# Layer 1's experts as a sorted, grouped product instead of a dense one, in a two-layer transformer kernel

## The chip, the cores and the metric

The kernel runs on one core of one Trainium2 chip. A core has TensorE (matrix products, called PE in the profile; its weight loads are PEld), VectorE (DVE), ScalarE (ACT), GpSimd (POOL) and SyncE (SP, which issues transfers). Each engine works through its own queue in order, and semaphores tie the queues together. The metric is the device time of one execution in microseconds (us), smaller is better. The input is fixed.

## The reference, cut to what matters

The input x is 4 batches of 1024 tokens of 128 elements, in F32. Layer 0 adds a multi-query attention and a SwitchHead attention with expert-wise values and outputs; both kernels compute it in the same way. Layer 1 is a linear attention with exponential features and, beside it, a mixture of experts. Both read the same normalised xn:

```python
logits = xf @ gate_w + gate_b                 # 4096 tokens, 8 experts
top_w, top_i = top_k(logits, 2)
combine = (softmax(top_w)[:, :, None] * one_hot(top_i, 8)).sum(axis=1)
for e in range(8):
    h = gelu(xf @ w1[e] + b1[e])              # 128 -> 512
    out = out + combine[:, e:e+1] * (h @ w2[e] + b2[e])   # 512 -> 128
shared = gelu(xf @ ws1 + bs1) @ ws2 + bs2
x = x + attention(xn) + out + shared
```

Only two of the eight routed experts have a weight other than zero for a token.

## The kernel before, in words

`build` (L2203) runs three stages with a barrier between them, then stores x whole. `layer0` computes layer 0, layer 1's normalised input xnT (turned, tokens in columns) and the gates. In it the VectorE functions `choose_experts` and `mix` with the helper `top2` (L130) find the two experts and write `combine`, 128 x 32 tiles x 10. Its SyncE queue loads head weights (L643, L652) and each step's queries (L635) over 32 steps of some 80 us. `load_experts` (L1544) loads the weights of all nine experts (the shared one is the ninth) and splits w1 into an upper and a lower part. `main1` (L1572) is layer 1.

`main1` takes the batches one after the other, each in 18 slots u (`UNITS` = 2 x 9). A slot holds one expert unit, expert u % 9 on token block u // 9 of 512 tokens: `hidden` (L1793) in two halves of six split products (`matmul3`, L76: upper x upper, upper x lower, lower x upper, one pass each, on lines L79, L80 and L81), `gelu` on ScalarE (L2074), `output` (L1804) one slot later in plain F32 (two instructions each, L1810), `mix` on VectorE (L1964), which multiplies with the combine weights, and `add_mixed` on GpSimd (L2157), which adds to x.

The attention is dealt out by hand over the same slots: projections and values in slots 0 and 1, `key_peaks` in 2 to 5 and `query_peaks` in 6 to 9 (VectorE takes their maxima, L1901 and L1925), `key_halves` in 8, `key_features` in 9 to 12, `query_shift` in 10, which needs GpSimd's `square_q` of slot 9, `sum_keys` in 10 to 13, `query_features` in 13 to 16, `turn_kv` in 14 with VectorE's `mask_kv`, `weigh` in 15 and 17, each followed by VectorE's `divide` (L1957 to L1961) into oT, and `project`, in 17 and in slot 0 of the next batch. GpSimd's `add_attn` adds the result to x. GpSimd also splits the next batch's x (`lower_x`, slot 15).

TensorE's results go to a ring of three tiles (`Ring`, two banks each). `claim` takes the next tile and waits until the result that was in it three claims before has been taken out. So the order of claims ties TensorE to the readers of the tiles.

## Time and profile before

| | |
|---|---|
| median of 3 runs | 3594.96 us (3593.2 to 3598.66) |
| the profiled execution | 3593.13 us |
| its span, first to last instruction | 3591.4 us |
| TensorE busy / weight loads | 3299.4 us (92%) / 2311.3 us |
| VectorE, ScalarE, GpSimd busy | 2363.4, 1687.0, 1755.3 us |
| mean granted TensorE clock | 0.967 |
| DMA packets, bytes | 115927, 79.23 MB |

The busy time of an engine is the sum of its instructions' times, and a busy TensorE is not TensorE at its peak, since matmuls overlap. A view by stretch gives these times for a part of the span, with the clock that TensorE was granted there (1.00 is 2.4 GHz, 0.50 is 1.2 GHz). The columns of a view by stretch are: stretch, its us, then busy us and (count) of PE, PEld, DVE, ACT and POOL, the granted clock, the share of busy DMA engines, GB/s. In a view in order of time a row is start us, us, engine, line, operation, output<-inputs, shapes, count, and in brackets the idle time before it and who ended it. A view of lines groups instructions of one form, with their mean time, and with the engine's idle time before them and who ended it. Every time of the working is one of the profiled execution.

### The profile page before, as it was taken

The page shows a single profiled execution, that of the slowest core. Times are in us where ns is not written, and L with a number is a line of the kernel's source. Part 1 is how long each engine was busy: PE and PEld are TensorE (multiplying, and loading weights), DVE is VectorE, ACT ScalarE, POOL GpSimd, SP SyncE. Part 2 cuts the span into 40 slices and gives each one's busy share as a digit, 9 for nine tenths or more (in the row PEclk, how much of TensorE's full clock was granted, in tenths as well). Part 3 has the DMA queues.
Part 4 walks back from the last instruction along what each step waited for, and adds up shares of the span by engine and source line. Part 5 has one row for each costly group of instructions (what it writes and reads, how often), then busy time and mean ns, then how long its engine had stood idle before and what let it go on. Part 6 is the DMA issues. An engine that isn't in the chain of part 4 may idle for free. (4 is left out here: it accounts for less than half of the span.)

```text
span 3591.4 us, 53232 instructions
## 1 busy us (share of the span) xinstructions
PE 3299.4 (92%) x19284; PEld 2311.3 (64%) x19284; DVE 2363.4 (66%) x3586; ACT 1687.0 (47%) x2854; POOL 1755.3 (49%) x1986
## 2 busy tenths in 40 slices
PE   3899999999999999999999999999993799989897
PEld 2566666666666666666666666666662677777675
DVE  6777888787888888888888888877863212122221
ACT  1445544545554445555454544555551363534444
POOL 1466656566665566666566665665652212121111
PEclk6999999999999999999999999999996899999998
DMA  3000000001000110010000001100003000000000
GB/s 86 18 25 26 19 19 28 28 26 31 20 19 19 30 33 25 20 32 19 24 29 28 19 20 32 31 19 19 25 2 67 9 1 1 1 1 1 1 1 24
DMA packets 115927, 79.23 MB, mean 22 GB/s; under 512 B 28618, under 2 KB 104020, under 8 KB 115668
## 3 DMA queue, kind: packets, MB, share of 16 engines
q1 hardware_dynamic: 113364, 73.46, 7.6%
q10 hardware_dynamic: 2304, 2.36, 0.3%
q8 instruction: 157, 2.57, 0.3%
q14 instruction: 102, 0.84, 0.1%
HBM read 63.74 MB, written 12.06 MB: 21 GB/s over the span
## 5 line engine op out<-in xcount | busy, mean ns | idle before, releaser
L883 ACT ACTIVATE m_expA<-m_ring 128x512 f32<-128x512 f32 x1024 | 547.5, 602 | 420.5 <-PE m_ring L329 297.4
L1114 DVE TENSOR_REDUCE m_peaks<-m_ring 128x1 f32<-128x512 f32 x1024 | 653.0, 684 | 126.1 <-PE m_ring L254 119.0
L774 POOL TENSOR_TENSOR m_vprod<-m_vprod 128x512 f32<-128x512 f32 x256 | 333.5, 1303 | 622.0 <-DVE m_vprod L1127 620.7
L783 POOL TENSOR_TENSOR m_oprod<-m_oprod 128x512 f32<-128x512 f32 x256 | 327.8, 1280 | 328.5 <-DVE m_oprod L1187 328.2
L307 PE MATMUL m_ring<-m_probT,m_vs 128*128 128x256 f32 x2048 | 466.8, 381 | 1.7 <-ACT m_probT L864 1.7
L864 ACT ACTIVATE m_probT<-m_ring 128x512 f32<-128x512 f32 x512 | 284.3, 601 | 363.5 <-PE m_ring L295 333.8
L307 PEld LDWEIGHTS m_ring<-m_probT,m_vs 128*128 128x128 f32 x2048 | 391.2, 191 | 60.3 <-ACT m_probT L864 2.2
L1127 DVE TENSOR_TENSOR m_vprod<-m_ring,m_gate 128x512 f32<-128x512 f32 x512 | 341.4, 687 | 77.7 <-POOL m_vs L776 55.0
L1157 DVE TENSOR_REDUCE m_neg<-m_wide 128x1 f32<-128x1024 f32 x256 | 312.7, 1221 | 105.7 <-PE m_wide L81 105.4
L1187 DVE TENSOR_TENSOR m_oprod<-m_ring,m_go 128x512 f32<-128x512 f32 x512 | 347.0, 688 | 31.0 <-PE m_ring L81 16.5
L2161 POOL TENSOR_TENSOR k_x<-k_x,m_mixed 128x512 f32<-128x512 f32 x72 | 91.9, 1276 | 534.5 <-DVE m_mixed L1970 534.5
L2080 ACT ACTIVATE m_hT<-m_ring,l_b 128x512 f32<-128x512 f32 x288 | 182.7, 686 | 352.5 <-PE m_ring L81 352.3
L1970 DVE TENSOR_TENSOR m_mixed<-m_ring,k_combine 128x512 f32<-128x512 f32 x72 | 49.8, 692 | 450.7 <-PE m_ring L1810 450.7
L854 ACT ACTIVATE m_prob<-m_wide,m_neg 128x1024 f32<-128x1024 f32 x256 | 288.3, 1126 | 104.3 <-DVE m_neg L1157 104.3
L295 PE MATMUL m_ring<-k_ident,m_prob 128*128 128x128 f32 x2048 | 275.9, 277 | 26.9 <-DVE m_peaks L1114 26.1
L295 PEld LDWEIGHTS m_ring<-k_ident,m_prob 128*128 128x128 f32 x2048 | 233.0, 142 | 92.8 <-issue 66.3
L1810 PEld LDWEIGHTS m_ring<-l_w,m_hT 128*128 128x128 f32 x2304 | 273.6, 195 | 8.9 <-issue 2.7
L344 PE MATMUL m_sums<-m_expA,m_v 128*32 128x512 f32 x2048 | 275.1, 609 | 1.5 <-ACT m_expA L883 1.4
L1810 PE MATMUL m_ring<-l_w,m_hT 128*128 128x128 f32 x2304 | 274.2, 278 | 1.1 <-ACT m_qpT L2060 1.1
L79 PE MATMUL m_ring<-m_wvs,m_xs 128*128 128x512 f32 x512 | 237.2, 463 | 35.1 <-DVE m_oprod L1187 23.6
L254 PE MATMUL m_ring<-m_ks,m_qs 32*128 32x512 f32 x1024 | 229.4, 504 | 33.4 <-DVE m_qs L1106 28.5
L79 PE MATMUL m_wide<-m_xs,m_yT 128*128 128x512 f32 x512 | 231.0, 451 | 9.2 <-DVE m_qs L1146 5.7
(249 smaller groups left out, 6239.5 us busy)
## 6 DMA issues: line engine op xcount, KB each, us to landing
m_wraw<-in_v_w SPq DMA_DIRECT2D x32, 512.0 KB, 4.0
m_qf<-q_dram SPq DMA_DIRECT2D x128, 128.0 KB, 2.7
m_wraw<-in_o_w SPq DMA_DIRECT2D x32, 512.0 KB, 3.8
q_dram<-m_kf SPq DMA_DIRECT2D x24, 256.0 KB, 4.3
sums_dram<-m_sumsT ACTq DMA_DIRECT2D x128, 18.0 KB
m_o_in<-sums_dram SPq DMA_DIRECT2D x64, 32.0 KB
m_rden_in<-rden_dram SPq DMA_DIRECT2D x64, 32.0 KB
p_w<-in_w SPq DMA_DIRECT2D x1, 2048.0 KB, 8.3
```

Of the source, the lines that this page charges most:

```text
L79: pe.matmul(out, wh, xh, start=True, stop=False)
L295: last = pe.transpose(ps[:, c * P:(c + 1) * P], prob[t % 2][:, (4 * h + c) * P:(4 * h + c + 1) * P], ident[:, :])
L307: last = pe.matmul(ps[:, 0:2 * P], vs[n % 2][:, k, :], probT[g % 2][:, k, :], start=(k == 0), stop=(k == TPB - 1))
L774: vchain(pool.tensor_tensor(vprod[:, 0:512], vprod[:, 0:512], vprod[:, 512:1024], ALU.add))
L783: ochain(pool.tensor_tensor(op[:, 0:512], op[:, 0:512], op[:, 512:1024], ALU.add))
L854: act.activation(prob[t % 2][:, :], wide.home["scores", n, t][:, :], ACT.Exp, bias=neg[t % 2][:, :], accum_out=den[n % 2][:, t:t + 1]).the ...
L883: act.activation(expA[hh][:, c * 512:(c + 1) * 512], ring.home["scT", n, k, hh, c][:, :], ACT.Exp)\
L1114: v.tensor_reduce(peaks[:, t, hh, c:c + 1], ring.home["peaks", n, t, hh, c][:, :], AX.X, ALU.max)\
L1127: v.tensor_tensor(vprod[:, c * 512:(c + 1) * 512].rearrange("p (e d) -> p e d", e=4), ring.home["values", n, t, c][:, :].rearrange("p (e d ...
L1157: v.tensor_reduce(neg[t % 2][:, :], wide.home["scores", n, t][:, :], AX.X, ALU.max, negate=True)\
L1187: v.tensor_tensor(oprod[t % 2][:, c * 512:(c + 1) * 512].rearrange("p (e d) -> p e d", e=4), ring.home["outputs", n, t, c][:, :].rearrange ...
L1810: last = pe.matmul(ps[:, t * P:(t + 1) * P], hT[j % 2][:, k, t * P:(t + 1) * P], w2[:, e, k, :], start=(k == 0), stop=(k == HT - 1))
```

## The change

`load_experts` goes. In layer 0, `top2` keeps the two chosen ranks in `choice`, SyncE writes the normalised rows to `xn_dram` (`store_xo`) and fills the list `listed` (9984 rows of 128) with zeros. `main1` computes for each token and each of its two experts a place in that list, sorted by expert, each expert's part rounded up to groups of 256: `count_places` on TensorE counts with a triangular matrix, `rank_tokens` on VectorE sums up. GpSimd sends the rows to their places with indirect DMAs (`send_rows`, 64 of them of 128 rows of 512 bytes), and for each of 39 groups (`NG`) fetches the weights of the group's expert (`fetch_weights`, 128 rows of 4112 bytes) into one of five buffers. A group is loaded by SyncE, turned, multiplied with w1 in plain F32, put through gelu and multiplied with w2, and its answers are stored in DRAM. In the last batch GpSimd fetches each token's two answers (`fetch_answers`, 64 indirect DMAs) and VectorE adds them with their shares (`add_answers`). x is stored in eight parts.

The shared expert stays as it was, in slots 2, 4, 11 and 12 (hidden) and 6 and 14 (output) of each batch. `group_slots` gives the places of the groups: from slot 27, which is slot 9 of batch 1, one per slot, two in the even slots of batch 2. With NG = 39 they end in slot 4 of batch 3.

```diff
+GROUP = 2 * P
+NG = B * T * 2 // GROUP + EM - 1
+FIRST_SLOT, SLOTS, NW = 27, 18, 5
+SHARED_HID = {2: (0, 0), 4: (0, 1), 11: (1, 0), 12: (1, 1)}
+SHARED_OUT = {6: 0, 14: 1}
+ANSWERS = {10: 0, 11: 1, 12: 2, 13: 3, 15: 4, 16: 5}
...
+                sp.wait_ge(eye_ready, 4)
+                filled = listed.rearrange("(p k) d -> p (k d)", p=P)
+                for k in range(0, NG * GROUP, ES * P):
+                    cols = min(ES * P, NG * GROUP - k)
+                    sp.dma_start(filled[:, k:k + cols], oprod[1][:, 0:cols]).then_inc(xo_stored, 16)
...
+def group_slots():
+    at, k = {n: [] for n in range(B * SLOTS)}, 0
+    for n in range(FIRST_SLOT, B * SLOTS):
+        for _ in range(2 if 2 * SLOTS <= n < 3 * SLOTS and n % 2 == 0 else 1):
+            if k < NG + 2:
+                at[n].append(k)
+                k += 1
+    return at
...
+                def load_rows(b):
+                    if b == 2:
+                        sp.wait_ge(rows_sent, 512)
+                    sp.dma_start(rows[:, 8 * (b % 2):8 * (b % 2) + 8, :], xn_dram[:, b * TPB:(b + 1) * TPB, :]).then_inc(loaded, 16)
...
+                def claim_front(k):
+                    claim(("front", k), *((y_kept, k - 1) if k >= 2 else (xgT_kept, k + 1)))
...
+                def group_hidden(j):
...
+                    pe.wait_ge(weights_loaded[j % 2], 16 * (j // 2 + 1))
+                    pe.wait_ge(xgT_kept, j + 1)
+                    ps = claim(("group hid", j), hg_ready, j + 1)
+                    for k in range(HT):
+                        last = pe.matmul(ps[:, k * GROUP:(k + 1) * GROUP], wg[j % NW][:, k * P:(k + 1) * P], xgT[j % 2][:, :],
+                                         start=True, stop=True)
+                    last.then_inc(hg_made, 1)
...
+                def group_output(j):
...
+                    pe.wait_ge(hg_ready, j + 1)
+                    ps = ring.home["front", j + 2][:, 512:1024]
+                    for h in range(2):
+                        for k in range(HT):
+                            last = pe.matmul(ps[:, h * P:(h + 1) * P], hg[j % 2][:, k, h * P:(h + 1) * P],
+                                             wg[j % NW][:, HID + k * D:HID + (k + 1) * D], start=(k == 0), stop=(k == HT - 1))
+                    last.then_inc(y_made, 1)
...
                 for b in range(B):
-                    for u in range(UNITS):
-                        hidden(b, u, 0)
-                        if u:
-                            output(b, u - 1)
-                        elif b:
-                            output(b - 1, UNITS - 1)
-                        hidden(b, u, 1)
+                    for u in range(SLOTS):
...
+                            if b == 0:
+                                count_places()
+                        if u in SHARED_HID:
+                            hidden(b, *SHARED_HID[u])
+                        if u in SHARED_OUT:
+                            output(b, SHARED_OUT[u])
...
+                        for k in slots[SLOTS * b + u]:
+                            claim_front(k)
+                            turn_group(k)
+                            group_output(k - 2)
+                            group_hidden(k - 1)
...
+                def add_answers(q):
+                    v.wait_ge(attn_added, q + 1)
+                    v.wait_ge(x_mixed, q + 1)
+                    v.wait_ge(answers_loaded[q % 2], 128 * (q // 2 + 1))
+                    for c in range(2):
+                        for t in range(4 * q, 4 * q + 4):
+                            last = v.scalar_tensor_tensor(out=x[:, t, :], in0=rows[:, 8 * (q % 2) + 2 * (t % 4) + c, :],
+                                                          scalar=shares[:, c, t:t + 1], in1=x[:, t, :],
+                                                          op0=ALU.mult, op1=ALU.add)
...
+                        if b == 0 and u == 1:
+                            rank_tokens()
...
+                        if b == B - 1 and u in ANSWERS:
+                            add_answers(ANSWERS[u])
                 divide(B - 1, 1)
-                mix(B - 1, UNITS - 1)
+                add_answers(2 * B - 2)
+                add_answers(2 * B - 1)
...
+                def send_rows(t):
+                    if t == 2 * TPB:
+                        pool.wait_ge(loaded, 16 * (n_loads + 2))
+                    for q in range(2):
+                        pool.indirect_dma_start(listed[:, :], bass.IndirectOffsetOnAxis(place[:, q, t:t + 1], 0),
+                                                rows[:, t % 16, :], None).then_inc(rows_sent, 16)
...
+                        if b == 0 and u == 1:
+                            for j in range(NW):
+                                fetch_weights(j)
+                        if b == 0 and 1 < u:
+                            for t in range(2 * u - 4, 2 * u - 2):
+                                send_rows(t)
+                        for k in slots[SLOTS * b + u]:
+                            if k + NW - 2 >= NW:
+                                fetch_weights(k + NW - 2)
+                        if b == B - 1 and u in ANSWERS:
+                            fetch_answers(ANSWERS[u])
                 add_attn(B - 1, 1)
-                add_mixed(B - 1, UNITS - 1)
+                fetch_answers(2 * B - 2)
+                fetch_answers(2 * B - 1)
```

`rank_tokens` begins with `v.wait_ge(rank_made, 1)` and is a chain of 27 VectorE instructions on tiles of 32 x 8, 39 x 8 and 8 x 16 elements per partition, each of which waits for the one before; the last one signals `ranked`, for which `fetch_weights(0)` and the release of the ring tile `places` wait. `fetch_answers(q)` issues eight indirect DMAs.

## Rows read from the trace of the kernel before

**Rows 1.** View in order of time, between the layers: start us, us, engine, line, operation

```profile
2766.59 0.39 SPq L1554 DMA_DIRECT2D p_w<-in_w  x1
...
2775.74 2.56 DVE L65 CAST l_w<-p_w 128x4608 fp32r<-128x4608 f32 x1 [9.44 <-DMA p_w<-in_ws]
...
2797.04 2.34 POOL L69 TENSOR_TENSOR m_xh<-k_xnT,m_xh 128x1024 fp32r<-128x1024 f32 x1 [0.24 <-ACT m_xh L2012]
...
2799.52 0.77 PE L79 MATMUL m_ring<-m_xh,l_w 128*128 128x512 f32 x1 [38.13 <-POOL m_xh L69]
```

**Rows 2.** Busy us of each engine by stretch, first and last of four batches

```profile
2799.50:2996.00 196.50, 181.92 (x1435) 144.74 (x1436) 43.86 (x48) 91.74 (x118) 32.97 (x24) 0.98 0.00 1
...
3385.00:3580.00 195.00, 180.70 (x1428) 144.57 (x1427) 43.53 (x48) 89.23 (x115) 31.90 (x24) 0.96 0.00 1
```

**Rows 3.** TensorE's waits in layer 1: us in total, times, longest

```profile
PE m_ring L79 <- DVE m_oT L1961: 29.6, 7, 5.6
```

**Rows 4.** TensorE in order of time: start us, us; layer 1, then layer 0

```profile
3018.41 0.50 PE L79 MATMUL m_ring<-m_xh,l_w 128*128 128x512 f32 x1 [0.28 <-ACT m_hT L2080]
...
3019.91 3.74 PE L1810 MATMUL m_ring<-l_w,m_hT 128*128 128x128 f32 x32
...
3023.40 0.48 PE L79 MATMUL m_ring<-m_xh,l_w 128*128 128x512 f32 x1
...
2994.41 0.79 PE L79 MATMUL m_ring<-m_xh,l_w 128*128 128x512 f32 x1 [5.62 <-DVE m_oT L1961]
...
2685.59 1.03 PEld L295 LDWEIGHTS m_ring<-k_ident,m_prob 128*128 128x128 f32 x8
...
2696.89 3.32 PEld L307 LDWEIGHTS m_ring<-m_probT,m_vs 128*128 128x128 f32 x16
```

**Rows 5.** The chain that ended last, layer 1: start us, us, what

```profile
2817.83 3.57 PE m_ring L1810 x32
...
2825.81 3.57 PE m_ring L1810 x32
...
2889.16 3.57 PE m_ring L1810 x32
...
2904.30 3.57 PE m_ring L1810 x32
```

**Rows 6.** Forms by line, layer 0: busy us, mean ns, idle before

```profile
L69 DVE TENSOR_TENSOR m_ctxT<-m_ring,m_ctxT 128x256 fp32r<-128x256 f32 x122 | 51.6, 423 | 137.9 <-ACT m_ctxT L874 136.6
...
L874 ACT ACTIVATE m_ctxT<-m_ring 128x256 fp32r<-128x256 f32 x122 | 47.0, 386 | 240.9 <-PE m_ring L307 240.9
```

**Rows 7.** One VectorE form in order of time, GpSimd busy, then idle

```profile
2718.78 1.18 DVE L143 SCALAR_TENSOR_TENSOR m_t_q<-m_t_sel,m_lg 128x64 f32<-128x64 f32 x1
...
2762.97 0.23 DVE L143 SCALAR_TENSOR_TENSOR m_t_q<-m_t_sel,m_lg 128x64 f32<-128x64 f32 x1
```

**Rows 8.** Forms by line, layer 1: busy us, mean ns, idle before

```profile
L2161 POOL TENSOR_TENSOR k_x<-k_x,m_mixed 128x512 f32<-128x512 f32 x72 | 91.9, 1276 | 534.5 <-DVE m_mixed L1970 534.5
...
L1901 DVE TENSOR_REDUCE m_peaks<-m_ring 128x16 f32<-128x1024 f32 x32 | 37.7, 1220 | 28.4 <-PE m_ring L1657 28.4
...
L2041 ACT ACT_TABLE_LOAD x16 | 20.5, 1283 | 0.3
...
L1958 DVE RECIPROCAL m_oden<-m_oden 128x512 f32<-128x512 f32 x8 | 26.8, 3353 | 0.3
```

**Rows 9.** The end in order of time

```profile
3582.28 0.39 SPq L2221 DMA_DIRECT2D out<-k_x  x1
```

**Rows 10.** SP in order of time, layer 0's query load of step 1

```profile
114.71 1.70 SPq L635 DMA_DIRECT2D m_qf<-q_dram  x4
```

**Rows 11.** Busy us by stretch, early in layer 0

```profile
40.00:80.00 40.00, 5.12 (x12) 2.95 (x12) 36.26 (x62) 2.99 (x4) 3.31 (x2) 0.50 0.16 46
```

**Rows 12.** Busy us by stretch in the last batch, around a wait

```profile
3540.00:3545.00 5.00, 1.81 (x14) 0.79 (x7) 4.20 (x3) 3.82 (x4) 0.00 (x0) 0.87 0.00 0
...
3545.00:3548.00 3.00, 3.00 (x11) 2.52 (x10) 0.00 (x0) 0.71 (x2) 0.00 (x0) 0.50 0.02 5
```

More of the change, by code:

```diff
@@ L127, in norm_memory, with top2, choose @@
     return {"bn": m.sbuf("bn", [P, NT, 6])} | {k: m.sbuf(k, [P, NT]) for k in ("mean", "rstd", "va", "t1", "y")}
-def top2(v, chain, p, tmp, order):
-    sel, c, q, m, first = (tmp[k] for k in ("sel", "c", "q", "m", "first"))
-    ob = order.unsqueeze(1).to_broadcast([P, m.shape[1], 8])
-    def choose(src, peak):
+def top2(v, chain, p, tmp, order, picks):
+    sel, c, q, first = (tmp[k] for k in ("sel", "c", "q", "first"))
+    ob = order.unsqueeze(1).to_broadcast([P, first.shape[1], 8])
+    def choose(src, peak, m):
         chain(v.tensor_reduce(peak, src, AX.X, ALU.max))
@@ L1340, in choose_experts @@
                     v.wait_ge(lg_kept, b + 1)
-                    one, other = top2(v, mx, lg[:, :, :], tmp, order[:, :])
+                    one, other = top2(v, mx, lg[:, :, :], tmp, order[:, :], [choice[:, q, b * TPB:(b + 1) * TPB] for q in range(2)])
                     mx(v.tensor_tensor(one, one, other, ALU.add))
@@ L1591, in main1 @@
         oden, oT = m.sbuf("oden", [P, 512]), m.sbuf("oT", [P, 512])
-        hT = [m.sbuf(f"hT{k}", [P, HT, 512]) for k in range(2)]
+        hT = m.sbuf("hT", [P, HT, 512])
         mixed = [m.sbuf(f"mixed{k}", [P, 4, D]) for k in range(2)]
         cT, extra = m.sbuf("cT", [EM + 2, 512]), m.sbuf("extra", [P, 4, D])
+        answers = nc.dram_tensor("answers", (NG * GROUP, D), F32, kind="Internal").ap()
+        earlier, thresholds = rank[:, 0:P], rank[:, P:P + 16]
+        numbers, lane = rank[:, P + 16:P + 16 + NG], rank[:, P + 16 + NG:P + 17 + NG]
@@ new lines, in main1 @@
+        place_f, place = m.sbuf("place_f", [P, 2, NT]), m.sbuf("place", [P, 2, NT], U32)
+        shares, owner = m.sbuf("shares", [P, 2, NT]), m.sbuf("owner", [P, NG])
+        weight_rows = m.sbuf("weight_rows", [P, NG], U32)
+        cum, begin = [m.sbuf(f"cum{k}", [P, 4 + EM]) for k in range(2)], m.sbuf("begin", [P, EM])
+        rows = m.sbuf("rows", [P, 16, D])
+        wg = [m.sbuf(f"wg{k}", [P, 2 * HID + HT]) for k in range(NW)]
+        xg, xgT = [m.sbuf(f"xg{k}", [P, 2, D]) for k in range(2)], [m.sbuf(f"xgT{k}", [D, GROUP]) for k in range(2)]
@@ L1610, in main1 @@
             "biased_made bias_added")
-        UNITS = 2 * (EM + 1)
+        rank_made, ranked, rows_sent, stored = m.sems("rank_made ranked rows_sent stored")
+        groups_turned, xgT_kept, hg_made, hg_ready, y_made, y_kept, xg_loaded, y_stored, answers_added = m.sems(
+            "groups_turned xgT_kept hg_made hg_ready y_made y_kept xg_loaded y_stored answers_added")
+        weights_loaded, answers_loaded = (m.sems(f"{n}0 {n}1") for n in ("weights_loaded", "answers_loaded"))
+        slots = group_slots()
         with nc.Block() as block:
@@ new lines, in claim_front, with turn_group @@
+                def claim_front(k):
+                    claim(("front", k), *((y_kept, k - 1) if k >= 2 else (xgT_kept, k + 1)))
+                def turn_group(j):
+                    if j >= NG:
+                        return
+                    turned_at = ring.home["front", j]
+                    pe.wait_ge(xg_loaded, 16 * (j + 1))
+                    if j:
+                        pe.wait_ge(xgT_kept, j)
+                    for k in range(2):
+                        last = pe.transpose(turned_at[:, k * P:(k + 1) * P], xg[j % 2][:, k, :], ident[:, :])
+                    last.then_inc(groups_turned, 1)
@@ L2103, in _ @@
                 for b in range(B):
-                    for u in range(UNITS):
-                        gelu(b, u, 0)
-                        gelu(b, u, 1)
+                    for u in range(SLOTS):
                         if u == 0:
@@ L2112, in _ @@
                             keep_combine(b, 0)
+                        if u in SHARED_HID:
+                            gelu(b, *SHARED_HID[u])
                         if u == 3:
@@ L2132, in _ @@
                             keep_out(b, 0)
+                        for k in slots[SLOTS * b + u]:
+                            group_gelu(k - 1)
                 keep_out(B - 1, 1)
```

356 lines of the change are left out of this document (244 added, 112 removed).

## The prediction

> **What bounds the kernel now.** I read the page first: TensorE is busy in nine tenths of nearly every slice. The views by stretch and by line then say what it is busy with. Layer 0 fills the span to 2766 us and the change leaves its arithmetic alone. Layer 1's matmuls begin at 2799.5 us [rows 1] and run to 3580 us: four batches of 195 to 196.5 us, each with TensorE busy for about 181 us, at a granted clock of 0.96 to 0.98 [rows 2]. In a batch VectorE is busy 44 us, ScalarE 90 and GpSimd 33, so TensorE's queue is the bound of layer 1, and the waits confirm it: TensorE's longest repeated wait is for m_oT, 29.6 us in 7 waits [rows 3].
>
> The 72 units (9 experts by 8 blocks) are most of that queue. One output product takes 3.49 us from its start to the next matmul [rows 4]; with its two hidden halves of 1.5 us [rows 4] a unit is 6.5 us, which two neighbouring slots bear out: 7.98 us apart, with only key peaks beside the unit [rows 5]. So the experts take 72 x 6.5 = 468 us of 780, and the attention 312 us, 78 per batch, of which some 11 us are waits. The attention is uneven: the slot from 2889.16 to 2904.30 us has 15.1 - 6.5 = 8.6 us of it [rows 5], a key-peak slot 1.5 us.
>
> **The change part by part.** *Experts removed and replaced.* 64 routed units go: 64 x 6.5 = 416 us less. The shared expert stays, 2 units or 13 us per batch. A group of 256 rows has two transposes (8 take 1.03 us, so 0.26 us), four hidden products with 256 moving columns in plain F32, two instructions each (16 such take 3.32 us, so 8 take 1.7 us), and an output half the size of a unit's (16 instructions, 1.8 us) [rows 4]: 3.77 us in all, 39 x 3.77 = 147 us added. Note what is saved and what isn't: the rows fall from 36864 to 9984 + 4096, but the hidden product goes from split to plain F32, four passes where three stood. TensorE's balance is -416 + 147 = -269 us. If that was all, layer 1 would end at about 3311 us. The rest of the sum is what the expert work had been covering.
>
> *The start.* The stage that loads and splits all experts goes. Now it loads from 2766.59 us and casts at 2775.74, main1's own constants follow after it, and the x split begins at 2797.04 us [rows 1]. After it, 15 constants and two row blocks (2.3 MB, like the 2.3 MB that landed in 9 us) are in by 2778.5 us; then cast, GpSimd's two splits and the 2.34 us x split [rows 1], 1.3 us more than now for ws1. Layer 1 starts at 2785 us, 14.5 us sooner.
>
> *Batch 0, no groups in it.* Slots 0 and 1 take 9 us at a clock that starts low. Then VectorE runs rank_tokens, 27 chained instructions. 128x256 forms cost 0.42 us and 128x64 forms 0.23 us [rows 6, 7]; with the chain's gaps I take 0.45 us each, 12.5 us (6 to 16). It stands ahead of key_max in VectorE's queue, and the ring has three tiles of which `places` holds one, so TensorE waits behind it. Key peaks then go at VectorE's pace, 8 x 1.22 us [rows 8] = 10 us; query peaks with one output product 14 us; 5 us more lead to query_shift: TensorE could be there at 50 us.
>
> GpSimd can't. Its queue holds, after `ranked` (21.5 us), 5 weight fetches and, from slot 2, 4 indirect sends per slot; the square for query_shift stands behind 28 sends. No trace row shows an indirect DMA. Let c be GpSimd's time for one. The nearest rows are an SP issue, 0.39 us [rows 1], from below, since there hardware writes the list, and a GpSimd pass over 128x512, 1.28 us [rows 8]; from above a 128x1024 pass, 2.34 us [rows 1]. I take c = 1.2 us, nearest to the instruction that also walks 128 partitions on the same engine, and keep both ends. The square is ready at 21.5 + 33 x 1.2 + 3.2 (one add, the square) = 64 us. From there the batch needs 55 us (in the trace 90 us from 2904.30 to the next batch's first product [rows 4, 5], less 7 units of 6.5 us, plus 10 us for the rest of slot 10, a hidden and an output product), and 5 us for waits that expert work used to cover and for the clock. Batch 0: 124 us. Its other GpSimd path, 57 DMAs to the next x split with one stall of about 7 us where sends wait for the second half of the rows, gives 38 + 57 x 1.2 = 107 us and isn't last.
>
> *Batch 1* has groups in its second half: 78 + 13 + 9 turns, 8 hidden and 7 outputs (28.5 us) + 2 = 122 us.
>
> *Batch 2* has 27 groups: 78 + 13 + 102 = 193. Nine slots hold two groups. In them the second group's output product needs a gelu that was only just released: four 128x256 activations at 0.39 us [rows 6] and a table load of 1.28 us [rows 8], 2.8 us of which nearly nothing is covered; 9 x 2.8 = 25 us more. The wait for m_oT at its borders is now covered by groups, -5. Batch 2: 213 us. Weight transfers (0.53 MB a group, five buffers, a group every 7 us) need 75 GB/s and stay hidden.
>
> *Batch 3.* Five slots of leftover groups (17 us), then attention alone: 58 us to the point in slot 10 where GpSimd begins to fetch answers. From there 48 fetches stand in its queue for slots 10 to 16, and VectorE waits in each of these slots for the answers just asked for (`answers_loaded`) before it may do mask_kv and divide, for which TensorE waits. TensorE has about 40 us of work there, GpSimd 48 x 1.2 = 58. After the 48th: 4.5 us to landing and adding (eight 128x128 additions), 5 for the last divide (the reciprocal alone 3.35 us [rows 8]), 3 projection, 1 copy, 1.5 add_attn; then 16 more fetches (19 us), 2.5 landing, 2 adding, 4 for the last 256 KB store: 64c + 23.5 = 100 us. Before, the store of 2 MB began at 3582.28 us [rows 9] and ended the span 9 us later, so little is saved there.
>
> *Layer 0.* SP's queue gets 10 zero fills (5.1 MB) at about 49 us, before the query load of step 1, which isn't due before 114 us [rows 10]; the stretch 40 to 80 us has a DMA share of 0.16 [rows 11], so some 17 us of transfer fit: nothing. The four stores of xo wait for what VectorE normalised in the same step, while SP's next issue waits for later work: nothing, at most 3 us each. Extra outputs in top2 replace a temporary of the same size: nothing.
>
> *Sum.* Span: 2785 + 124 + 122 + 213 + 58 + 100 = 3402 us, 189 less than 3591.4. The profiled execution took 3593.1 us for that span, and the median is 1.9 us above it: 3406, a gain of 5.3%.
>
> **A rule weighed.** One VectorE form, the 128x64 scalar_tensor_tensor, took 1.18 us while GpSimd computed and 0.23 us while it stood idle [rows 7]. The new add_answers is of that form and runs beside GpSimd's fetches. The Trainium skill (SBUF — State Buffer, Practical consequences) says that a VectorE instruction with two SBUF inputs contends with a GpSimd instruction that reads SBUF and not with one that only writes it. By the row, the tail's additions cost 7 us more than I put down; by the page, if a fetch only writes descriptors, nothing. I keep it at nothing in the sum and inside the range.
>
> The Trainium skill (DMA: Bandwidth & Descriptors, Anatomy of one DMA — SWDGE (gpsimd) path) gives about 2.0 us fixed per such DMA, most of it completion. If all of it held GpSimd, an estimate from this page would be 0.8 x 97 = 78 us more, 3484; no run here shows it yet.
>
> **The rivals.**
> (A) *The clock falls in the thin stretches.* After 4 us of waiting in the last batch, the granted clock went from 1.0 to 0.50, the lower level, for the next stretch [rows 12]. In batch 0 and late in batch 3 TensorE waits often. If it is at the lower level for half of batch 0's 80 us and half of the first 58 us of batch 3, that adds about 50 us: 3455. For it: such a wait occurs anyway at each border; against it: in most slots the new waits are 1 to 3 us.
> (B) *GpSimd is not the bound.* c at 0.4 to 0.7 us: batch 0 ends 14 us sooner and batch 3 follows TensorE, about 45 us sooner: 3345.
> (C) *GpSimd is slower than taken,* c = 1.7 to 2.9. Each us of c costs 33 + 64 = 97 us, above c = 2 the x split comes last too and it is 121. At c = 2.3 this gives 3406 + 78 + 36 = 3520.
> (D) *Slower than before.* The same place, one mechanism: GpSimd's in-order queue in batches 0 and 3. 189 us are used up at c = 2 + (189 - 78)/121 = 2.9 us; at 3.3 us the time would be 3640. Against it: no GpSimd instruction of 128x512 in the trace takes half of that.
> The Trainium skill (SBUF — State Buffer, A bandwidth-pool intuition that's wrong) reports such a DMA at 0.62 us alone and 3.1 us under a VectorE copy, which would be D; VectorE's copies here read PSUM, and I leave D's chance at what the rows give.
>
> **How the numbers follow.** Forecast 0.60; A 0.13; B 0.08; C 0.13; D 0.05, and 0.01 for a result at no change. Range: from B's 3340 to C's 3525. Faster by over 0.2% (about what a measurement of this kernel can tell from no change): 0.60 + 0.13 + 0.08 + 0.13 = 0.94.
>
> **What the changed profile would show.** First matmul of layer 1 near 2785 us; a TensorE wait of 10 us for VectorE in slot 2 of batch 0; query_shift waiting for GpSimd's m_squares some 14 us; GpSimd's queue solid with indirect DMAs of 1.2 us at the start and end of layer 1; batch 2 at about 213 us with waits of about 3 us for m_hg; then VectorE waiting for m_rows, and TensorE for m_kvw and m_oT, in the last 100 us. Wrong would be: batch 2 far from 213 (the group's price), or batch 3's tail at another length than 64c + 23.5.

## The result and the profile after

The changed kernel takes 3484.68 us in the median of four runs (3480.67 to 3488.13), the kernel before 3596.81 (3593.2 to 3599.15): ratio 0.9689, 95% interval 0.9674 to 0.9703. It is faster by 112 us, where 189 were forecast. The profiled execution took 3482.56 us with a span of 3480.7.

The same view as [rows 1], the boundary between the layers, of the changed kernel (start us, us, engine, line, operation; in brackets the idle time before it and who ended it):

```profile
2772.55 0.36 SPq L1658 DMA_DIRECT2D m_wraw<-in_wkT  x1
...
2785.25 0.36 DVE L76 CAST m_wh<-m_wraw 128x384 fp32r<-128x384 f32 x1 [10.84 <-DMA m_rows<-xn_dram]
...
2788.24 2.52 POOL L80 TENSOR_TENSOR m_xh<-k_xnT,m_xh 128x1024 fp32r<-128x1024 f32 x1
...
2791.01 0.77 PE L90 MATMUL m_ring<-m_xh,m_wh 128*128 128x512 f32 x1 [23.66 <-POOL m_xh L80]
```

Layer 1 starts at 2791.0 us, 8.5 sooner than before and 6 later than forecast: SyncE issues its first constant 6 us later than in [rows 1]. Other kernels below with the same layer 0 start it as early as 2784.8 us (e6_small), so these 6 us are the spread of layer 0 and not a cost of the change.

To cut layer 1 into batches I use one instruction of VectorE that stands near the start of each, m_v (L2097, 6 to 8 us after the first matmul of layer 1). It starts at 2797.4, 2958.1, 3085.4 and 3290.7 us. From one to the next, batch 0 takes 160.7 us, batch 1 127.3, batch 2 205.3, and 190.0 remain from the last one to the end (196.6 if counted like the forecast's batch 3, from the first matmul). The stretches between these points, with busy us of each engine, granted clock, DMA share and GB/s; it answers to [rows 2]:

```profile
core 0: us, PE busy (x) PEld busy (x) DVE busy (x) ACT busy (x) POOL busy (x), PEclk, DMA share, GB/s
2791.00:2958.00 167.00, 109.06 (x764) 70.25 (x765) 42.70 (x60) 38.91 (x44) 82.58 (x79) 0.73 0.15 49
2958.00:3085.00 127.00, 108.18 (x923) 78.24 (x922) 39.58 (x48) 61.43 (x84) 19.66 (x17) 0.95 0.16 47
3085.00:3291.00 206.00, 179.74 (x1440) 144.24 (x1439) 55.13 (x87) 92.12 (x161) 39.96 (x37) 0.99 0.35 104
3291.00:3481.00 190.00, 104.92 (x814) 70.02 (x812) 53.58 (x104) 40.25 (x56) 70.25 (x72) 0.75 0.14 38
```

Batches 1 and 2, which have groups and few indirect DMAs, are within 8 us of the forecast (122 and 213). The time is missing in the first and the last batch (124 and 158 forecast), where GpSimd issues the sends and the fetches. GpSimd's indirect DMAs by line (busy us, mean ns of one, idle us before them):

```profile
L2391 POOL DMA_INDIRECT listed<-m_rows,m_place x64 | 62.2, 971 | 19.1 <-issue 18.2 <-POOL k_x L2422 0.6 <-POOL k_x L2383 0.3
L2414 POOL DMA_INDIRECT m_rows<-answers,m_place x64 | 60.6, 947 | 26.3 <-issue 18.3 <-DVE k_x L2084 7.2 <-POOL k_x L2383 0.3
```

0.97 us of work and 0.30 of issue: one costs GpSimd 1.27 us, where 1.2 was taken. So c is not the miss. What is new stands in the waits. The waits of VectorE and ScalarE in layer 1 whose end no record explains, which the profile calls "remote" (us in total, times, longest):

```profile
DVE m_veps L2134 <- remote: 60.7, 2, 40.3
...
DVE m_qmax L2126 <- remote: 21.3, 4, 9.1
...
DVE m_oden L2158 <- remote: 20.2, 2, 13.8
...
ACT m_hT L2288 <- remote: 41.3, 2, 26.2
...
ACT m_kshT L2240 <- remote: 24.3, 1, 24.3
...
ACT m_qpT L2268 <- remote: 21.2, 1, 21.2
...
ACT m_kp L2247 <- remote: 17.5, 3, 16.7
```

And TensorE in one such stretch, in order of time, while GpSimd issues 16 sends from 2880.39 to 2899.50 us:

```profile
2884.33 0.64 PE L1791 MATMUL m_kv_sums<-m_kp,m_v 128*32 128x256 f32 x8
2884.77 0.60 PE L1791 MATMUL m_kv_sums<-m_kp,m_ones 128*32 128x256 f32 x4
2886.06 1.11 PE L1791 MATMUL m_kv_sums<-m_kp,m_ones 128*32 128x256 f32 x4 [0.69 <-issue]
2887.50 0.48 PE L1801 MATMUL m_small<-m_eps,m_v 128*128 128x1 f32 x3 [0.34 <-issue]
...
2888.93 0.49 PE L1801 MATMUL m_small<-m_eps,m_v 128*128 128x1 f32 x3 [0.56 <-issue]
2890.38 0.41 PE L1801 MATMUL m_small<-m_eps,m_v 128*128 128x1 f32 x3 [0.95 <-issue]
...
2896.79 0.59 PE L92 MATMUL m_ring<-m_xh,m_w 128*128 128x512 f32 x1 [0.82 <-issue]
...
2899.62 0.79 PE L92 MATMUL m_ring<-m_xh,m_w 128*128 128x512 f32 x1 [0.83 <-issue]
```

Read the start times. Up to 2885 us a dozen matmuls start within half a microsecond. Then the tiny products with one moving column (value_sums, 16 of them) start one to three at a time, some 0.7 us apart, and a pass of a split product waits up to 0.8 us for "issue", that is for nothing that the profile shows. Between the 16 products the program has no wait for a semaphore, so they start late for no reason that it gives. From 2903.2 us on, 3 us after the last send, a dozen start each microsecond again.

TensorE's signals are late too. VectorE's copy m_veps waits, in batch 0, for the value_sums products alone. Below are the last of them and the copy in the changed kernel, then the copy in e1_none, a kernel of the next section without the sends, whose last such product starts at 2872.9 us and takes 0.25 us:

```profile
2893.97 0.37 PE L1801 MATMUL m_small<-m_eps,m_v 128*128 128x1 f32 x1 [0.55 <-issue]
...
2903.39 0.16 DVE L2134 COPY m_veps<-m_small 128x1 f32<-128x1 f32 x1 [40.27 <-remote]
```

```profile
2873.14 0.16 DVE L2133 COPY m_veps<-m_small 128x1 f32<-128x1 f32 x1 [19.70 <-PE m_small L1800]
```

Without the sends the copy follows at once; in the changed kernel it starts 9.0 us after the product's end. The packed trace has the times of the semaphores: this signal came at 2903.36 us. Of the 354 signals that TensorE gives in layer 1, 28 came 1.1 to 27.7 us after the recorded end of their product, and in e1_none none came over 0.1 us after it. All the waits listed above as "remote" are for products of TensorE, so here the word stands for its late signals, and the readers that they hold back hold TensorE back in turn. Whether the products were done late or only reported late, the trace does not tell. I call both, the late starts and the late signals, late service of TensorE.

### The profile page after: what moved, and what is told of

It reads as the page before. It is cut to its first block and busy times, and to the rows that moved or that the text cites. A ratio compares the mean times of both kernels' runs of the same rounds, so it can differ in the third digit from the quotient of the medians.

```text
span 3480.7 us, 49858 instructions
## 1 busy us (share of the span) xinstructions
PE 3082.9 (89%) x17486; PEld 2102.0 (60%) x17486; DVE 2385.8 (69%) x3698; ACT 1552.7 (45%) x2731; POOL 1823.8 (52%) x2090
## 3 DMA queue, kind: packets, MB, share of 16 engines
q0 software_dynamic: 9712, 28.93, 2.8%
## 5 line engine op out<-in xcount | busy, mean ns | idle before, releaser
L90 PE MATMUL m_ring<-m_wvs,m_xs 128*128 128x512 f32 x512 | 237.3, 464 | 34.1 <-DVE m_oprod L1216 23.6
L265 PE MATMUL m_ring<-m_ks,m_qs 32*128 32x512 f32 x1024 | 229.5, 505 | 33.3 <-DVE m_qs L1133 28.5
L340 PE MATMUL m_ring<-m_qs,m_ks 32*128 32x512 f32 x1024 | 217.7, 489 | 3.0 <-DVE m_vprod L1154 2.6
L90 PE MATMUL m_ring<-m_wos,m_ctxT 128*128 128x512 f32 x512 | 216.7, 423 | 0.6 <-ACT m_expA L910 0.6
L811 POOL TENSOR_TENSOR m_oprod<-m_oprod 128x256 f32<-128x256 f32 x256 | 197.2, 770 | 20.1
L92 PE MATMUL m_ring<-m_wvs,m_xs 128*128 128x512 f32 x512 | 206.3, 403 | 0.0
L91 PE MATMUL m_ring<-m_wvs,m_xs 128*128 128x512 f32 x512 | 205.0, 400 | 0.0
```

Source lines behind the costliest of these rows:

```text
L90: pe.matmul(out, wh, xh, start=True, stop=False)
```

## The experiments

Layer 1 begins up to 10 us earlier or later from kernel to kernel, so I compare the stretch from m_v of batch 0 to the end of the span ("layer 1" below): 683.3 us for the changed kernel. All but e11_early and e12_both_b were executed once; five executions of e11_early lie within 7.3 us, so a difference of that size between two kernels is not one. The theories at first were **S**: while indirect DMAs follow one another closely, TensorE is served late; **Q**: GpSimd's in-order queue holds up its squares and additions; **C**: the attention without expert work beside it is that slow by itself. In the expectations "160.7 us" is from m_v to m_v, though the first of them says otherwise, and "196" from the first matmul of batch 3; my figures for the last stretch are from m_v, 190.0 us for the changed kernel.

**Without sends and fetches** (e1_none):

```diff
-   for q in range(2):
-       pool.indirect_dma_start(listed[:, :], ..., rows[:, t % 16, :], None)
...
-   for t in range(4 * q, 4 * q + 4):
-       for c in range(2):
-           pool.indirect_dma_start(rows[:, ...], None, answers[:, :], ...)
```

> Leaves out the 64 sends of rows and the 64 fetches of answers (the answers are not those of the reference then); the ranking, the 39 groups and their weight fetches stay. Theory S (starved: while GpSimd issues indirect DMAs one behind the other, TensorE's instructions reach it 0.4 to 2 us apart): batch 0, which took 160.7 us from the first matmul of layer 1 to m_v of batch 1, falls to 115 to 125; batch 3 with the tail, 196 us, to 135 to 150; the kernel to 3375 to 3400. Theory Q (GpSimd's own queue: its squares and additions stand behind the DMAs): the same, since the queue is empty too. Theory C (thin work at a low clock: the attention without groups takes that long by itself): batch 0 stays above 145 and the kernel above 3450.

Measured: 3374.18 us. Its batches:

```profile
2791.50:2922.40 130.90, 100.94 (x764) 69.38 (x765) 42.61 (x60) 38.68 (x44) 20.51 (x15) 0.78 0.07 22
2922.40:3049.80 127.40, 108.59 (x926) 79.37 (x925) 39.58 (x49) 61.43 (x84) 19.96 (x16) 0.95 0.16 47
3049.80:3255.00 205.20, 178.94 (x1433) 143.43 (x1432) 54.70 (x86) 92.12 (x161) 39.13 (x37) 0.99 0.35 105
3255.00:3372.00 117.00, 91.11 (x818) 62.76 (x816) 53.52 (x104) 40.14 (x56) 10.05 (x8) 0.91 0.09 26
```

From m_v to m_v batch 0 takes 122.8 us (the first row starts 8.2 us earlier, at the first matmul), batches 1 and 2 are unchanged to 0.1 us, and the last takes 117.3, less than expected. So the 128 DMAs cost 38.0 + 72.7 = 110.7 us, and C falls: the thin batches run at 0.78 and 0.91 of the clock with nothing else beside them and are still that much shorter.

**GpSimd as busy, but no DMA** (e2_stand):

```diff
-   pool.indirect_dma_start(listed[:, :], ..., rows[:, t % 16, :], None).then_inc(rows_sent, 16)
+   pool.memset(scratch[:, :], 0.0).then_inc(rows_sent, 1)      # scratch 128x1360
```

(the same for the fetches, each memset behind the one before it)

> Each of the 64 sends and 64 fetches is replaced by a memset of 128x1360 on GpSimd, by the rate of its memsets 1.25 us, the pitch of the indirect DMAs: GpSimd is as busy in the same places, but no DMA is issued. S: TensorE is served as usual, batch 0 115 to 130 us, kernel 3390 to 3415. Q: batch 0 stays at 155 to 165, batch 3 with the tail at 190 or more, kernel 3475 to 3490. C: as Q.

Measured: 3430.85 us, between what S and Q expected. One memset took 1.23 us. The first and the last stretch, from m_v, whose exact lengths are 132.3 and 165.2 us:

```profile
2799.00:2931.00 132.00, 95.02 (x734) 62.35 (x733) 42.30 (x59) 37.59 (x43) 97.12 (x78) 0.78 0.09 30
...
3264.00:3429.00 165.00, 94.01 (x816) 63.63 (x815) 54.53 (x104) 40.16 (x56) 88.73 (x72) 0.80 0.06 18
```

GpSimd is busy 97 us of 132 there, and no wait is "remote". So both theories hold in part. The queue costs 57.5 us over e1_none, 9.5 of them in batch 0 and 47.9 in the last stretch. The rest to the changed kernel is 53.2 us, 28.5 in batch 0 and 24.9 at the end (51.7 between the spans, since layer 1 began 1.5 us apart). GpSimd's occupancy, which is the same here, does not make that difference by itself. But this kernel also has a tile more, scratch, and the last run shows that such a tile may matter.

**One DMA at a time** (e3_spaced):

```diff
+   if t or q:
+       pool.wait_ge(rows_sent, 16 * (2 * t + q))
    pool.indirect_dma_start(listed[:, :], ..., rows[:, t % 16, :], None).then_inc(rows_sent, 16)
```

(the same before each fetch)

> Each send and each fetch of an answer waits until the one before it has landed, so no two are under way; the pitch goes from 1.27 to about 2.3 us. S, if it is their close order that starves TensorE: no stretch in which its instructions come 0.7 us and more apart; batch 0 is then bound by GpSimd's 64 x 2.3 = 147 us and some 20 us of other work, 160 to 175, and the kernel is at 3480 to 3515. Q: 64 x 1.05 = 67 us more in batch 0 (about 225) and some 50 us more behind the last group, kernel 3580 to 3610.

Measured: 3580.54 us, Q's number. The pitch became 2.56 us ((62.2 us of work + 101.5 of waits) / 64). But batch 0 took 177.2 us, near S's 160 to 175 and far from Q's 225; no wait is "remote", and value_sums of batch 0 runs in 1.7 us. The end takes 255.9 us, 66 more: there, the queue decides, and a longer pitch is paid in full.

**Plain DMAs of the same rows** (e4_direct):

```diff
-   pool.indirect_dma_start(listed[:, :], bass.IndirectOffsetOnAxis(place[:, q, t:t + 1], 0),
-                           rows[:, t % 16, :], None).then_inc(rows_sent, 16)
+   pool.dma_start(listed[at:at + P, :], rows[:, t % 16, :]).then_inc(rows_sent, 16)
```

> The 64 sends and 64 fetches of answers become plain GpSimd DMAs of the same 128 rows to and from fixed places (the rows are not sorted then). S, if it is the indirect form (descriptors made from 128 indices) that starves TensorE: the gaps go, batch 0 115 to 130, kernel 3385 to 3415. S, if it is any DMA that GpSimd issues in close order: batch 0 150 to 165, kernel 3465 to 3490. Q: by the pitch of the plain DMAs alone; at one of 1.27 us as now, 160 us and 3480.

Measured: 3388.48 us, batch 0 122.8 us and nothing "remote". A plain DMA holds GpSimd 0.54 us, so this is a queue of less than half the length. It moves as many packets and bytes on the software queue as the changed kernel (9712 packets, 28.93 MB), faster, and TensorE isn't served late. What traffic the rows make is not the cause.

**Plain DMAs at the old pitch** (e5_padded): the kernel above with a memset of 128x800 behind each DMA.

> Plain DMAs of 128 rows to and from fixed places as in e4_direct, each followed by a GpSimd memset of 128x800 (about 0.73 us), so that GpSimd is busy for about 1.27 us for each, as with the indirect ones; the same bytes and packets at nearly the same pace (the rows are not sorted). If the indirect form itself starves TensorE: as with the memsets alone, e2_stand, 3425 to 3440 us, batch 0 130 to 135 us from m_v to m_v. If it is 128 packets every 1.27 us in whatever form: as the changed kernel, 3475 to 3490, batch 0 155 to 163.

Measured: 3430.99 us, batch 0 130.5, nothing "remote": 0.14 us from e2_stand. A second way of holding GpSimd for 1.27 us, this time with all the traffic, costs what the first did. The queue's price is 57 us whatever fills it, in two kernels that both have the scratch tile.

**Sixteen rows for 128** (e6_small):

```diff
-   bass.IndirectOffsetOnAxis(place[:, q, t:t + 1], 0), rows[:, t % 16, :]
+   bass.IndirectOffsetOnAxis(place[0:16, q, t:t + 1], 0), rows[0:16, t % 16, :]
```

> The 128 sends and fetches stay indirect, but each moves 16 rows in place of 128 (the other 112 rows are left out). If the cost lies in what one indirect DMA costs whatever its size, its pitch stays at 1.27 us, TensorE's gaps stay and the kernel is at 3470 to 3490. If it lies in the 128 rows (a descriptor made for each), either the pitch falls and the kernel comes to 3385 to 3410, or the pitch stays and the gaps go, 3425 to 3440.

Measured: 3489.98 us, layer 1 697.7 us, 14.4 more than with 128 rows. One takes 0.84 us of GpSimd in place of 0.97, so the pitch is 1.14. An eighth of the rows saves an eighth of the time: the price is that of the instruction. It still makes as many packets on the software queue (9712), with 21.59 MB in place of 28.93, so the rows fell and the packets did not. And late service did not go with the rows. Layer 1 is longer although the queue is shorter; the "issue" time before value_sums grew from 9.1 to 14.9 us, while the "remote" waits of VectorE and ScalarE fell from 208 to 99 us in all. The 16 matmuls of value_sums of batch 0 (ns of one, first and last start us, and below it the idle time ahead of them in us, times), first in the changed kernel, then in this one, then in e1_none:

```profile
L1801 PE MATMUL m_small<-m_eps,m_v x16: 163/250/371, 2887.5 to 2894.0; 128*128 128x1 f32 x16
its engine sat idle before it (us, times) until:
  issue: 9.1, 15
```

```profile
L1801 PE MATMUL m_small<-m_eps,m_v x16: 163/352/353, 2896.6 to 2904.8; 128*128 128x1 f32 x16
its engine sat idle before it (us, times) until:
  issue: 14.9, 13
```

```profile
L1800 PE MATMUL m_small<-m_eps,m_v x16: 250/250/271, 2871.2 to 2872.9; 128*128 128x1 f32 x16
its engine sat idle before it (us, times) until:
  issue: 0.4, 1
```

**The sends spread** (e7_sends): 64 sends over slots 2 to 26.

```diff
-   if b == 0 and 1 < u:
-       for t in range(2 * u - 4, 2 * u - 2):
-           send_rows(t)
+   n = SLOTS * b + u - 2
+   for s in range(64 * n // 25, min(64, 64 * (n + 1) // 25)) if n >= 0 else ():
+       send_rows(s // 2, s % 2)
```

> Only the 64 sends are spread: 2 or 3 in each of the 25 slots from slot 2 on, in place of 4 in each of 16 slots; all are still out before the first group. S: with 3.3 us of DMAs in a slot of 6 to 7 us neither the queue nor the close order delays TensorE: from m_v to m_v batch 0 falls from 160.7 to 125 to 138, batch 1 rises from 127 to no more than 135, kernel 3450 to 3468. If the indirect DMAs cost TensorE a time each wherever they stand: batch 0 falls to about 145 and batch 1 rises to about 142, kernel 3475 to 3490.

Measured: 3452.62 us; batch 0 129.3 and batch 1 134.5, as expected: of the 38 us that the sends cost, 24 are back. (Layer 1 is at 659.4 us, 23.9 less; it began 6 us sooner, which is the rest of the difference in the whole time.)

**Groups sooner and fetches spread** (e8_spread):

```diff
-   for _ in range(2 if 2 * SLOTS <= n < 3 * SLOTS and n % 2 == 0 else 1):
+   for _ in range(2 if n < 3 * SLOTS and n % 2 == 0 else 1):
...
-   if b == B - 1 and u in ANSWERS:
-       fetch_answers(ANSWERS[u])
+   if b == B - 1 and u >= 1:
+       for t in range(2 * u - 2, min(NT, 2 * u)):
+           fetch_answers(t)
```

(with `ADDS = {4: 0, 6: 1, 8: 2, 10: 3, 12: 4, 14: 5}` for VectorE's additions)

> The spread sends, and in batch 3: two groups also in the even slots of batch 1 (the last group is done in slot 0 of batch 3 and not in slot 4), 4 fetches of answers in each slot from 1 to 16 in place of 8 in each of six slots and 16 behind the last addition, and the additions of a quarter two slots behind its last fetch, so that VectorE finds the rows there. Batch 1 grows by some 15 us for its four added groups, batch 3 loses them. S: batch 3 with the tail falls from 190 to 145 to 160 and the kernel is at 3410 to 3445. Against it: 4 fetches are 5.1 us in a slot of 6 to 7 us, close enough to starve TensorE in batch 3 all the same; then batch 3 stays above 165 and the kernel is at 3450 to 3470.

Measured: 3452.23 us, a miss; layer 1 654.0 us, only 5.4 less than e7_sends. The last stretch fell from 189.1 to 151.3 us, 16 of it for the four groups moved, but batch 1 rose by 29 us to 163.3, where four groups explain 16. And in the last stretch "remote" waits remain, 30.3 us for m_veps alone. Nothing ties GpSimd's queue to the slots. Its fetches went out in runs of 20 and 12, not in fours.

**GpSimd held to the slots** (e9_paced):

```diff
+   def keep_pace(b, u):
+       for first, last, sem in ((2, 5, k_max), (6, 9, q_max), (10, 12, k_exp), (13, 16, q_exp)):
+           if first <= u <= last:
+               pool.wait_ge(sem, 8 * b + 2 * (u - (9 if sem is k_exp else first)) + 1)
```

> e8_spread with one thing more: in each slot GpSimd waits for the peaks or the exponentials of that slot before it issues the slot's DMAs. In e8_spread nothing held it back, and its 64 fetches went out in runs of up to 20 behind one another. S: with at most 4 in a row and a pause behind them TensorE is served in between; batch 3 with the tail falls from 151 to 125 to 142 and the kernel from 3452 to 3425 to 3443. Against it: if what counts is how many indirect DMAs lie in a stretch and not how they are bunched, batch 3 stays at 148 to 158 and the kernel at 3450 to 3460.

Measured: 3423.85 us, layer 1 626.3 us, 27.7 less than e8_spread; the last stretch takes 138.7. Waits that only hold GpSimd back made the kernel faster.

**A memset between the DMAs** (e10_pause): the changed kernel with a memset of 128x600 behind each send and fetch.

> The changed kernel with a memset of 128x600 (about 0.55 us) behind each send and each fetch of answers, which makes their pitch 1.85 us, between the 1.27 us at which TensorE's instructions trickled and the 2.56 us of e3_spaced at which they didn't. If the trickle needs the closest order: value_sums of batch 0 runs as without the DMAs (1 us), batch 0 is bound by GpSimd's queue at 145 to 158 us and the kernel is at 3470 to 3505. If it remains at this pitch: its gaps come on top of the longer queue, batch 0 is at 170 or more and the kernel at 3520 to 3560.

Measured: 3475.65 us, layer 1 678.1 us. The pitch is 1.75 us (2829.69 to 2831.45 and on), GpSimd has 79 us more to do, and the kernel is not slower than the changed one: layer 1 is 5.2 us shorter, which is too little to count between single executions. Nothing is "remote"; value_sums of batch 0 takes 1.7 us. I took this for proof that the close order is the cause. The last run showed that this proof doesn't hold.

**All groups done in batch 2** (e11_early): e9_paced with two groups in every slot but the last of a batch, three fetches in each of slots 49 to 70.

```diff
-   for _ in range(2 if n < 3 * SLOTS and n % 2 == 0 else 1):
+   for _ in range(1 if n % SLOTS == 17 else 2):
```

> e9_paced with two groups in every slot from 27 on but the last slot of a batch, so that all 39 are done in slot 47 of 72 (in batch 2), and the 64 fetches are spread over slots 49 to 70, three in each, the additions of a quarter behind them. S: GpSimd issues 3.8 us of indirect DMAs in a slot of 6 to 7 us, as in the sends of e7_sends, which cost 7 to 14 us in all; with some 10 us for the fetches the kernel is at 3385 to 3415, faster than the changed kernel by 70 to 100 us. Against it: if the thin stretch without groups (now 24 slots) runs at a lower clock than the same work beside groups, it costs more than it gives, 3430 to 3460; if each indirect DMA costs TensorE a time wherever it stands, 3430 to 3450.

Measured: 3426.85 us (3421.34 to 3428.64), ratio to the kernel before 0.9527 (0.9514 to 0.9540); as e9_paced, and not the 3385 to 3415 expected. The last stretch fell by 19 us, to 120.1, and batch 1 rose by 22. In its two-group slots TensorE waits for the gelu, as in the changed kernel (below), 27.9 us in all, where e9_paced has 18.9 and the changed kernel 13.0.

**Both** (e12_both_b): e11_early with the memset of e10_pause behind each fetch.

> e11_early with the memset of 128x600 of e10_pause behind each of the 64 fetches: three of them are then 5.6 us in a slot of 6 to 7 us, at a pitch of 1.85 us, at which TensorE was served without gaps. If what is left of the trickle costs e11_early time (its fetches still go out in runs of 9 and 18 at 1.27 us), the stretch from m_v of batch 3 to the end falls from 120 to 108 to 117 us and the kernel to 3405 to 3422. If the trickle is gone already and GpSimd's queue counts, the added 37 us of its time make it 3428 to 3445.

Measured: 3416.41 us (3411.33 to 3420.43), ratio to the kernel before 0.9494 (0.9481 to 0.9507): the fastest version, 68 us below the changed kernel. Its time was expected; the place was not. The last stretch did not fall (123.2 us). What fell is batch 1, from 178.6 to 171.8, where this kernel's program does not differ from e11_early's: its memsets stand behind the fetches only, which begin in batch 2. Here are three of its sends in batch 0, of a run of 20 with only an addition between them:

```profile
2831.00 0.96 POOL L2404 DMA_INDIRECT listed<-m_rows,m_place  x1 [0.30 <-issue]
2832.27 0.97 POOL L2404 DMA_INDIRECT listed<-m_rows,m_place  x1 [0.30 <-issue]
2833.54 0.97 POOL L2404 DMA_INDIRECT listed<-m_rows,m_place  x1 [0.30 <-issue]
```

1.27 us apart, as in the changed kernel; 24 more stand in one run from 2922.2 to 2954.1 us. And not one wait of VectorE or ScalarE in its layer 1 is "remote". So close order alone does not make TensorE late. This rests on the one profile of this kernel; its five executions (3411 to 3420 us) were all faster than the five of e11_early (3421 to 3429).

What the kernels have in common: every one with "remote" waits (the changed kernel, e6_small to e9_paced, e11_early) issues indirect DMAs in close order and has no scratch tile. e2_stand, e5_padded, e10_pause and e12_both_b have one, of 800 to 1360 columns or of 600, declared behind rows; it moves the tiles declared after it in SBUF (the groups' weights, inputs and answers), and these kernels also have more instructions in GpSimd's program. None of them has a "remote" wait. Of the kernels without it, e1_none, e3_spaced and e4_direct have none either. The chip is not what they differ in: e6_small to e8_spread, with late service, and e5_padded and e12_both_b, without it, ran on the same one. So in these runs late service came only with indirect DMAs, in close order, in kernels without the scratch tile, and it was gone when any of the three was changed: plain DMAs in e4_direct, a pitch of 2.56 us in e3_spaced, the tile in e12_both_b. That memsets of 1.27 us would leave TensorE alone without the tile was not tested. Whether the tile's shift in SBUF or the place of the instructions matters, and what it is that is late (the fetch of instructions, or something else), stays open. The run that would tell, the changed kernel with an unused tile of 128x600 and nothing else, was not made; if the tile's shift is all, it should give about e2_stand's 3431 us, which is an estimate.

## Why the prediction was right and wrong

**Right: the direction, the range and the bound.** 3484.7 lies in 3340 to 3525, and GpSimd's queue does cost time at the start and the end of layer 1, as forecast: that is the difference of e2_stand to e1_none. Its size was right too: the forecast less rival B is 3406 - 3345 = 61 us (14 in batch 0, some 45 at the end), and e2_stand less e1_none is 56.7, 9.5 and 47.9 by place. c was 1.27 us for 1.2 taken. Ranking took 10.4 us, from 2800.13 to 2810.50, for 12.5. That the time lies in the range is luck in part. The range went up to 3525 for a c of up to 2.3 us; c was as taken, and what filled that room, 52 and 29 us, is in no term of the sum.

**The groups.** One output product and one hidden product in batch 2, and a transpose:

```profile
3147.16 2.05 PE L1933 MATMUL m_ring<-m_wg,m_hg 128*128 128x128 f32 x16 [1.44 <-ACT m_hg L2299]
3149.04 1.89 PE L1922 MATMUL m_ring<-m_xgT,m_wg 128*128 128x256 f32 x8
3150.87 1.15 PE L1736 MATMUL m_ring<-m_proj,m_qT 32*128 32x256 f32 x16
...
3153.33 0.44 PE L1912 MATMUL m_ring<-k_ident,m_xg 128*128 128x128 f32 x2 [0.34 <-DVE m_qmax L2126]
3153.60 1.95 PE L1933 MATMUL m_ring<-m_wg,m_hg 128*128 128x128 f32 x16
```

From start to start: 1.88 + 1.83 + 0.27 = 3.98 us a group, 3.77 forecast. The hidden product was put at 1.7, from a row of weight loads (PEld) in [rows 4]. Twenty-seven of them make batch 2 5.7 us longer, and yet it was 8 us shorter than 213: the gelu wait of a two-group slot was taken at 2.8 us and is 1.44. TensorE's waits in batch 2, which answer to [rows 3]:

```profile
PE m_ring L1933 <- ACT m_hg L2299: 13.0, 9, 1.5
PE m_ring L1868 <- DVE m_oT L2162: 3.7, 1, 3.7
```

13.0 us for 25. The step that failed is that four activations and a table load lie bare; the hidden product of another group and the slot's attention cover half of them.

**Wrong: 52 us that were in no term.** The forecast has GpSimd's DMAs as time in GpSimd's queue and nothing else. That they can make TensorE late while its semaphores are all met stands in no row of the kernel before, which has no indirect DMA. The changed kernel's 3480.7 less e2_stand's 3429.0 is 51.7 us, with the reservation on e2_stand's extra tile. In batch 0 it also hides the queue: query_shift was to wait 14 us for GpSimd's square, which was ready at 2861.1 us, 70 us after the start (64 forecast). But TensorE's own products before it came late, and it started at 2872.6 us without a wait for the square. In e2_stand, where they are in time, TensorE waits 7.1 us there, until the square is ready. The profile calls that wait "issue" as well, so the word alone proves no late service; that takes the program, which has no wait between the value_sums products.

**Wrong: 29 us in the thin batches.** e1_none has neither queue nor late service and corresponds to rival B, 3345 us; it took 3374. By place: the start 6.5 us (the spread of layer 0, as said), batch 0 122.8 for 110, batch 1 127.4 for 122, batch 2 205.2 for 213, the last 125.5 for 113 (counted from the first matmul). The two thin ones are 12.8 and 12.5 us longer than worked out from the attention of the kernel before. Their clock is 0.78 and 0.91, a mix of its two levels (1.2 and 2.4 GHz), where I had kept the 0.96 to 0.98 of [rows 2] but for 5 us. That is rival A in part, at perhaps half of its 50 us; how much of the 25 us is clock and how much are waits that the experts had covered, I did not test.

**The end.** Forecast 64c + 23.5, with the measured c 104.8 us; from the first fetch (3351.3) to the end it took 129.4. The last lines, which answer to [rows 9], fit the sum by steps:

```profile
3451.17 1.26 POOL L2430 TENSOR_TENSOR k_x<-k_x,m_extra 128x512 f32<-128x512 f32 x1 [9.74 <-ACT m_extra L2280]
3452.70 0.96 POOL L2414 DMA_INDIRECT m_rows<-answers,m_place  x1 [0.27 <-POOL k_x L2430]
...
3471.44 0.94 POOL L2414 DMA_INDIRECT m_rows<-answers,m_place  x1 [0.30 <-issue]
3474.07 2.31 DVE L2084 SCALAR_TENSOR_TENSOR k_x<-m_rows,m_shares,k_x 128x128 f32<-128x128 f32 x8 [7.72 <-DMA m_rows<-answers,m_place]
3476.41 0.37 SPq L1687 DMA_DIRECT2D out<-k_x  x1
```

16 fetches in 20 us, 1.7 to the landing, 2.3 of additions, 4.3 for the store. The 25 us over the sum lie before them: the difference to e2_stand in this stretch is 24.9.

**The rules weighed.** Eight additions that run while GpSimd issues fetches (from 3410.2 to 3429.9 us) take no longer than the eight behind the last fetch, 2.33 for 2.31 us or 0.29 each, and not the 1.18 of [rows 7]:

```profile
3423.71 2.33 DVE L2084 SCALAR_TENSOR_TENSOR k_x<-m_rows,m_shares,k_x 128x128 f32<-128x128 f32 x8
```

The Trainium skill (SBUF — State Buffer, Practical consequences) says that a GpSimd instruction that only writes does not contend with such an addition; the trace agrees if a fetch is counted as one. The Trainium skill's 2.0 us fixed for a DMA from GpSimd (DMA: Bandwidth & Descriptors, Anatomy of one DMA — SWDGE (gpsimd) path) gave 3484 us, which is the measured time by accident: GpSimd is held 1.27 us, and the rest came from the late service and the thin batches. That page gives most of the 2.0 us to completion, and where the landing is waited for, in e3_spaced, the pitch is 2.56 us.

## What to carry to other kernels

An engine that issues DMAs is a term of the sum twice: as time in its own queue, and as what its DMAs do to engines that wait for nothing. The second shows only as "issue" and "remote" in the waits; where they appear beside a run of indirect DMAs, first pace the run by the consumers' semaphores (28 us here) before changing the work. Put as few indirect DMAs as possible where no arithmetic covers them, since the price is that of the instruction and hardly of its rows, and replace one, as a test, by an equally long instruction of the same engine: that tells the queue's price in one run. If the test needs a tile or more instructions, give the kernel that it is compared with the same ones; here the test brought a tile with it, and the tile turned out to be a suspect itself.

## What the runs showed of the hardware

- An indirect DMA of 128 rows of 512 bytes holds GpSimd 0.95 to 0.97 us, and 0.30 us of issue follow; one of 16 rows 0.84. A plain one of the same bytes takes 0.54.
- Beside indirect DMAs at pitches of 1.14 and 1.27 us TensorE was late, in kernels without the scratch tile: 14.9 and 9.1 us of "issue" in 16 products that otherwise have 0.4. VectorE and ScalarE then wait "remote", 208 us in all in the changed kernel, for signals of TensorE that come up to 27.7 us after the recorded end of their products; GpSimd's own instructions keep their time. At 2.56 us there is none, and with the scratch tile none at 1.27 either.
- DMA load is not what it depends on: the share of the DMA engines was 0.15 in batch 0, and beside plain DMAs of the same bytes in less time no wait was "remote".
- Waits put in front of GpSimd's DMAs took 27.7 us off, and 79 us of added memsets did not make the kernel slower (layer 1 678.1 us for 683.3).
- Layer 0, the same in all these kernels, ended up to 10 us apart (m_v of batch 0 from 2790.5 to 2800.5 us); a comparison of single executions should start behind it.
